# Who issues the row-maximum DMAs of a fused attention kernel: SyncE before, ScalarE after

## The reference

```python
scores = jnp.einsum('bhid,bhjd->bhij', Q, K) / scale
QJ = jnp.einsum('bhid,hde->bhie', jnp.tanh(Q), J_attn)
delta = jnp.einsum('bhie,bhje->bhij', QJ, jnp.tanh(K))
scores = scores + lambda_attn * delta
scores = jnp.where(causal, -jnp.inf, scores)
probs = jax.nn.softmax(scores, axis=-1)
out = jnp.einsum('bhij,bhjd->bhid', probs, V)
```

## Time and profile before

| what | us |
|---|---|
| median of 3 runs | 2716.73 |
| lowest and highest | 2701.98, 2717.15 |
| the profiled execution's span | 2717.9 |
| attention stage (to about) | 1560 |
| PE busy, over the span | 2166.4 (80%) |
| ACT busy, over the span | 1021.0 (38%) |
| DVE busy, over the span | 1310.0 (48%) |

### The profile page before, as it was taken

One profiled execution on the slowest core, in us unless ns is written; L12 is line 12 of the kernel. 1 busy time (PEld: TensorE's weight loads), 2 busy tenths in 40 slices (PEclk: granted clock), 3 DMA queues, 4 the chain that ended last, 5 costly groups with the idle time before them and its releaser, 6 DMA issues. The chain is left out here.

```text
span 2717.9 us, 46428 instructions
## 1 busy us (share of the span) xinstructions
PE 2166.4 (80%) x12830; PEld 1526.6 (56%) x12831; DVE 1310.0 (48%) x2904; ACT 1021.0 (38%) x1784; POOL 748.0 (28%) x1097
## 2 busy tenths in 40 slices
PE   3677787787769777877797738788999999998784
PEld 1344455454446444544465426676777777776674
DVE  4544454454435444544464454443444444444665
ACT  1233342443334333433353312224555555554221
POOL 3112221222123122212231226655600000001775
PEclk8678988888889788988898768898999999999897
DMA  8886857776776668576966244334411111112675
GB/s 220 153 130 140 176 130 131 141 164 134 139 150 157 121 147 168 144 132 143 173 147 123 84 158 142 129 115 137 147 54 54 56 54 56 54 54 93 218 242 170
DMA packets 225152, 358.67 MB, mean 132 GB/s; under 512 B 28240, under 2 KB 114256, under 8 KB 224976
## 3 DMA queue, kind: packets, MB, share of 16 engines
q1 hardware_dynamic: 205776, 309.02, 49.3%
q0 software_dynamic: 15744, 46.16, 5.1%
q10 hardware_dynamic: 3456, 1.34, 0.2%
HBM read 210.92 MB, written 144.44 MB: 131 GB/s over the span
## 5 line engine op out<-in xcount | busy, mean ns | idle before, releaser
L602 DVE TENSOR_REDUCE mx<-ps_rows 128x1 f32<-128x128 f32 (+3 forms) x1024 | 478.2, 486 | 440.5 <-PE ps_rows L452 424.0
L553 ACT ACTIVATE probs<-ps_cols 128x1024 f32<-128x1024 f32 (+3 forms) x512 | 357.9, 699 | 656.2 <-PE ps_cols L465 655.7
L465 PE MATMUL ps_cols<-qs,ks 98*128 98x512 f32 (+3 forms) x1024 | 316.2, 393 | 225.7 <-DMA qs<-mT 225.6
L450 PE MATMUL ps_rows<-ks,qs 96*128 96x128 f32 (+3 forms) x1024 | 436.8, 428 | 70.8 <-issue 25.3
L736 POOL TENSOR_TENSOR pace<-eps 1x1 f32<-1x1 f32 x256 | 48.5, 190 | 1037.2 <-ACT probs L553 1037.2
L465 PEld LDWEIGHTS ps_cols<-qs,ks 98*128 98x128 f32 x1024 | 178.1, 217 | 230.7 <-issue 184.2
L450 PEld LDWEIGHTS ps_rows<-ks,qs 96*128 96x128 f32 x1024 | 215.0, 210 | 146.9 <-issue 71.2
L452 PE MATMUL ps_rows<-mask_bf,ident_bf 128*128 128x128 bf16 x1024 | 251.8, 246 | 0.0
L1709 DVE TENSOR_TENSOR h_lo<-ps_h,h_hi 128x512 fp32r<-128x512 f32 x135 | 93.4, 692 | 254.3 <-ACT h_hi L1681 254.3
L478 PE MATMUL ps_o<-probs,vt 128*32 128x512 f32 (+3 forms) x2048 | 197.8, 460 | 0.1
L452 PEld LDWEIGHTS ps_rows<-mask_bf,ident_bf 128*128 128x128 bf16 x1024 | 106.9, 104 | 148.7 <-issue 113.2
(11 more groups left out here) (204 smaller groups left out, 4135.8 us busy)
## 6 DMA issues: line engine op xcount, KB each, us to landing
ks<-k_parts SPq DMA_DIRECT2D x96, 256.0 KB, 9.3
qs<-q_parts SPq DMA_DIRECT2D x96, 256.0 KB, 12.6
ks<-k_parts SPq DMA_DIRECT2D x192, 128.0 KB, 4.5
qs<-q_parts SPq DMA_DIRECT2D x192, 128.0 KB, 6.6
xs_d<-zrows SPq DMA_DIRECT2D x45, 384.0 KB, 3.0
xr<-xs_d SPq DMA_DIRECT2D x135, 128.0 KB, 2.0
yo_d<-y_e SPq DMA_DIRECT2D x135, 128.0 KB, 1.7
xn<-in_L_attn_x_dram SPq DMA_DIRECT2D x16, 512.0 KB, 4.8
```

The costliest lines, as they stand in the source:

```text
L450: nc.tensor.matmul(bank[:, 0:(it + 1) * P], qs[0:STACK, hh, it * P:(it + 1) * P], ks[0:STACK, hh, 0:(it + 1) * P], start=True, stop=False)
L465: mm = nc.tensor.matmul(ps_cols[pair][:, e, jt * P:S], ks[0:MROW + 2, hh, jt * P:(jt + 1) * P], qs[0:MROW + 2, hh, jt * P:S], start=True, ...
L553: nc.scalar.activation(probs[:, n % 2, 2 * pair:2 * pair + 2, jt * P:S], ps_cols[pair][:, :, jt * P:S], ACT.Exp).then_inc(exp_done, 1)
L602: nc.vector.tensor_reduce(mx[:, gb, it, h:h + 1], ps_rows[h % 2][:, 0:(it + 1) * P], AX.X, ALU.max)\
```

## The change

ScalarE issues the four DMAs itself, directly behind its copy to `mT`, and waits first for the completion of that copy. SP's `max_rows` is gone, with its wait. The semaphore, its counts and who waits for it are as before.

```diff
                     nc.scalar.activation(mT[0:2 * HG], ps_m[0:2 * HG], ACT.Copy).then_inc(taken[kind], 1)
+                    act.wait_ge(taken[kind], count(kind, j, d))
+                    act.nop(nofuse=True)
+                    for h in range(HG):
+                        act.dma_start(qs[MROW:MROW + 2, slot(d, j) + h].bitcast(F32), mT[2 * h:2 * h + 2, :].bitcast(F32))\
+                            .then_inc(mrow_loaded, 16)
...
-        def max_rows(d, g):
-
-            sp.wait_ge(taken["mt"], d.v * G + g + 1)
-            sp.nop(nofuse=True)
-            for h in range(HG):
-                sp.dma_start(qs[MROW:MROW + 2, slot(d, g) + h].bitcast(F32), mT[2 * h:2 * h + 2, :].bitcast(F32)).then_inc(mrow_loaded, 16)
...
-                        elif kind == "mt":
-                            max_rows(d, j)
```

## The result

The changed kernel takes 2738.22 us (median of 4 runs, 2736.6 to 2748.78) against 2715.94 before: the ratio of the two is 1.0117, with a 95% interval of 1.0076 to 1.0159. It is slower, by 1.2%. Forecast was 2697, that is 0.7% faster; the time lies inside the range of 2665 to 2745, but on the other side of the kernel before. The profiled execution has a span of 2737.8 us against 2717.9.

What follows compares the result with a forecast made beforehand. PE's stream was taken to bound the kernel, with ScalarE and SP no bound. From the profiled 2717.9: - 46 - 4 + 24 + 6 = 2698, or 2697 against the median, 0.7% faster; range 2665 to 2745.

Steps and rivals of the forecast that it cites:

- What bounds, and what is late next: PE's stream bounds; after the row maxima at step 8, the query stack loads are late, needed at step 9, landing 625.9.
- The long wait: PE's wait at step 8 for the row maxima, 15 times, 221.75 us; expected to shrink to about 11 us each, renamed.
- The gain: Rest of step 8 runs at full clock before PE waits for the query stack: 15 x 3.1 = 46 us saved.
- The hold's length: ScalarE held 3.18 us from its copy's start by four DMA issues, next activation 2.7 us later, 64 times.
- The price of PE's wait: At step 13, PE's second `gt` piece starts 1.7 us later, counted in full: 14 x 1.7 = 24 us lost.
- the cover that I named: At step 9, PE at low clock in some 8 of 15 batches hides later `ont` copies: 6 of 12 us lost.
- -46 - 4 + 24 + 6: Step 8's rest at full clock, three step 0 waits gone, then losses at step 13 and step 9, in us.
- The rival that names the slower side: Small DMAs stay behind the backlog in shared DMA engines, landing past 622; holds remain: 2754, 1.3% slower; chance 0.13.
- a hold of more than 3.9 us instead of 3.2: ScalarE held longer by its issues would eat up the gain, at 29 us for each us.

## Why the prediction was wrong, point by point

**What bounds, and what is late next: right.** The long wait changed its name and went from 221.7 to 161 us in the 15 batches, and ends as the stack lands. That the small DMAs land in time through ScalarE's queue was right too: PE waited at most 1.7 us for them.

**The gain: the mechanism right, the size low.** 46 us were forecast and 64.7 came. Step 8's rest ran at full clock in all batches but one and took 45.8 us, 3.05 a batch (3.1 forecast). Most of the other 19 is the clock: from PE's restart to step 9's transposes the low clock lasted 108.3 us in the 15 batches before, and 72.5 after, and half of the difference, 18 us, is what the slower clock takes from busy time. I had let it last as long in both. Part of the 64.7 is scatter: with the six traces that have SP's order (505.5 us in the mean) set against the five in which ScalarE issues this set (448.5), the gain is 57.

**The hold's length: right.** 3.23 us against 3.18, and 1.61 us of waiting where 1.7 were forecast.

**The price of PE's wait: the step that failed.** The prediction put step 13's hold at "14 x 1.7 = 24 us", taking a wait to cost what it lasts ("it counts in full"). The wait was sized rightly; what was put at nothing without a reason is the clock behind it. The stretch lost 43.3 us, of which the waits for the gt copy are 21.5; PE's busy time rose by 30.4 for the same matmuls, about half of the 65 us that the low clock lasted longer, and the "issue" stalls fell by 10. The experiments carry this: a hold without DMAs costs the same, one of half the length nothing, and moving the piece that waits restores the clock while the hold stays.

**Step 9: the cover that I named wasn't there.** I took 6 of 12 us, since a lasting low clock would hide the rest. But in the kernel before the low clock was over by step 9's transposes in every batch (0.0 us in the stretches from there to step 13), so nothing was there to hide behind, and all 15 batches pay: 18.9 us, about 1 in each of 14 and 5.3 in the first, where 10.7 us ran at the low clock. The wait that came is not that of the `out` piece for the `ont` copy either: PE's `cols` waits some 0.7 us for the exponentials that stand behind the hold on ScalarE, 10.1 us in all. With step 9's set alone the stretch pays the same.

**The last batch: left out.** I had walked through the four places of one batch in the steady state. Batch 15 has no projections of a next batch; its groups take 12 us, not 16 to 22. That this leaves less work on PE to cover a hold of 3.2 us is my reading; no run tests it by itself. It lost 18.9 us, with 37.5 us at the low clock where there had been none.

With the low clock left out, the holds were priced at 30 us and cost 81. In the sum: -65 + 43 + 19 + 19 + 3.5 = +20 instead of -46 - 4 + 24 + 6 = -20. That the time still lies inside the range is in part luck: the gain came out 19 us larger than forecast and hid a part of the 51 us that the holds cost more. The rival that names the slower side was not what happened (the maxima weren't late); the time it gave, 2754, is near by chance. The sentence beside it, that "a hold of more than 3.9 us instead of 3.2" would eat up the gain, was the nearer one, but the hold was 3.2.

## What to carry to other kernels

When a wait is to be removed, look for when the next thing that its engine needs arrives; here that row set the size of the gain within a third. Then price the new holds on the engine that serves the bottleneck not by their length alone: follow them through every phase of the loop, the first and last iteration as well, and count what the clock does after the wait that they cause. And ask first whether the late instruction can simply stand earlier in its own queue; that took the gain here at no price.

## What the runs showed of the hardware that I had not expected

- Short waits of PE moved its granted clock. With waits of some 1.6 us at step 14, in 14 batches, the time at the low clock in the stretch behind rose from 108 to 173 us (changed kernel) and 176 us (hold without DMAs); with waits of 0.3 us it was 92. The clock fell at this place in 10 of those batches before the change too, with no wait or one of 0.5 us ahead of it, but always after the 16 matmuls of 8 columns each of the `lg` piece had begun, 7.6 to 10.7 us after the transposes. With the longer waits it fell in all 14, in 10 of them (13 with the hold without DMAs) before the `lg` piece began, 6.3 to 7.6 us after the transposes in the changed kernel. Why it falls at this place and not at others with waits as short stays open.
- The time at the low clock after the long wait was not fixed: 3.6 to 10.1 us before, 3.6 to 7.3 us after, for waits of 12.6 to 16.5 and near 11 us. The kernel with SP's order changed, waiting 7.5 to 11.2 us, had 3.6 to 10.9. What decides it in a single batch stays open.
- Four DMA issues of 4 KB took 2.38 us on ScalarE's queue and 2.42 to 2.44 on SP's; the median of the 256 issues was 571 ns there, the longest took twice that:

```profile
L545 ACTq DMA_DIRECT2D qs<-mT x256: 569/571/1175, 101.1 to 1528.7; - x128
```

- Small DMAs of ScalarE's queue landed ahead of large ones that SP had issued before them, while the 16 DMA engines were full (share 1.06 from 688 to 698). SP issued three stack loads from 687.65 on, which took 13.6 to 16.5 us to land, that is until 705.0; ScalarE issued the maxima from 688.83 to 691.2, and PE, which had waited 0.41 us for them, went on at 697.96.

```profile
688.83 2.38 ACTq L545 DMA_DIRECT2D qs<-mT  x4
...
L795 SPq DMA_DIRECT2D qs<-q_parts x3: 318/460/471, 687.7 to 688.5; - x3
...
DMA to landing us min/median/max: 13.6/15.0/16.5
```

The Trainium skill ("DMA: Bandwidth & Descriptors", "Queues, rings and completion order") has the engines take packets from each issuer's ring in turn. The trace agrees: loads issued ahead of the maxima landed at 701.3 to 705.0, behind them.
